# Prepare stage of a state-space and attention kernel: x split between the statistics pass and the first channel group, and filter taps made with the powers as the moving operand

## The reference

```
def _layernorm(x):   m = mean(x, -1); v = var(x, -1); return (x - m) / sqrt(v + 1e-5)
# first layer, a diagonal state-space model per channel d with 64 states n
A_bar = exp(DT * -exp(log_A));  B_bar = (A_bar - 1) / A * B_param
K[d, t] = sum_n C[d, n] * B_bar[d, n] * A_bar[d, n] ** t        # the filter taps
y = causal convolution of layernorm(x) with K, + D * layernorm(x);   x2 = x + y
# second layer: windowed attention, plus routed attention over 512 and 1024 chosen rows
```

## Time and profile before

| | us |
|---|---|
| Median of three runs | 4485.69 |
| Profiled execution: its time, its span | 4487.98, 4486.3 |
| Prepare block: 0 to first work of conv_phase | 144.0 |
| of it: to the start of taps and statistics | 11.3 |
| of it: loop of 32 steps | 11.3 to 121 |
| of it: end of the statistics, `krow`, store, end of block | 121 to 144 |
| conv_phase and what lies around it | 144 to about 620 |
| the rest | to 4486.3 |

### The profile page before, as it was taken

The page is one execution under the profiler, slowest core; times in us unless marked ns, Lnnn a source line. Parts: engine busy times, 40 slices in busy tenths (PEclk is TensorE's granted clock), DMA queues, the critical chain, the costliest instruction groups (busy, mean ns, idle before and its releaser), DMA issues. The chain is left out here.

```text
span 4486.3 us, 94318 instructions
## 1 busy us (share of the span) xinstructions
PE 4223.0 (94%) x37156; PEld 3557.5 (79%) x37156; DVE 2888.1 (64%) x4994; ACT 1852.9 (41%) x4838; POOL 869.6 (19%) x661
## 2 busy tenths in 40 slices
PE   9688879999999999999999999689999999999999
PEld 9577767888888888878888888577878777777777
DVE  7788867776676666755555666746465564655645
ACT  6334424343443434434444333225344453444534
POOL 0122202222222222222222222210110101111101
PEclk9999979999999999999999999869999999999999
DMA  9778852222222322212121211220210202112010
GB/s 306 217 201 230 225 160 76 90 79 89 83 90 82 90 86 84 79 50 65 58 67 58 63 62 46 90 57 6 50 40 21 55 8 50 25 36 46 16 42 13
DMA packets 341117, 369.20 MB, mean 82 GB/s; under 512 B 22848, under 2 KB 220736, under 8 KB 340672
## 3 DMA queue, kind: packets, MB, share of 16 engines
q1 hardware_dynamic: 262336, 295.91, 22.2%
q0 software_dynamic: 12288, 33.56, 3.6%
q10 hardware_dynamic: 66048, 33.56, 2.8%
HBM read 236.60 MB, written 76.02 MB: 70 GB/s over the span
## 5 line engine op out<-in xcount | busy, mean ns | idle before, releaser
L1685 POOL TENSOR_TENSOR l_prob<-l_prob,l_inv 128x768 f32<-128x768 f32 x256 | 389.6, 1543 | 1699.0 <-DVE l_inv L1642 1699.0
L1236 ACT ACTIVATE l_prob<-l_ps_s,l_neg_max 128x192 f32<-128x192 f32 x1024 | 420.7, 443 | 7.9 <-DVE l_neg_max L1618 7.7
L2296 DVE TENSOR_REDUCE h_neg_max<-h_ps_s 128x1 f32<-128x1024 f32 x256 | 312.8, 1222 | 166.6 <-PE h_ps_s L2082 163.4
L2217 ACT ACTIVATE h_prob<-h_ps_s,h_neg_max 128x1024 f32<-128x1024 f32 x256 | 285.5, 1115 | 292.5 <-DVE h_neg_max L2299 292.5
L1618 DVE TENSOR_REDUCE l_neg_max<-l_ps_s 128x4 f32<-128x768 f32 x256 | 233.1, 952 | 237.6 <-PE l_ps_s L1005 218.7
L2094 PE MATMUL h_ps_t<-ident,h_prob 128*128 128x128 f32 x2048 | 272.8, 276 | 14.4 <-ACT h_prob L2217 13.9
L2094 PEld LDWEIGHTS h_ps_t<-ident,h_prob 128*128 128x128 f32 x2048 | 228.3, 140 | 62.6 <-issue 27.7
L2106 PEld LDWEIGHTS h_ps_o<-h_probs_t,ahead_then_values 128*64 128x64 f32 x4096 | 220.9, 137 | 43.2 <-issue 37.0
L2106 PE MATMUL h_ps_o<-h_probs_t,ahead_then_values 128*64 128x128 f32 x4096 | 251.8, 276 | 0.0
L2353 DVE COPY h_probs_t<-h_ps_t 128x512 f32<-128x512 f32 x256 | 176.8, 691 | 115.8 <-PE h_ps_t L2094 114.3
L1236 ACT ACTIVATION_READ_ACCUMULATOR l_prob<-l_ps_s,l_neg_max 128x1 f32 x1024 | 235.2, 230 | 0.0
(11 more groups left out here) (384 smaller groups left out, 11222.3 us busy)
## 6 DMA issues: line engine op xcount, KB each, us to landing
xin<-in_L_attn_x_dram SPq DMA_DIRECT2D x32, 1024.0 KB, 5.1
xg<-in_L_attn_x_dram SPq DMA_DIRECT2D x64, 512.0 KB, 9.4
toep_back<-taps_padded ACTq DMA_DIRECT2D x32, 1024.0 KB, 10.6
x<-xg SPq DMA_DIRECT2D x64, 512.0 KB, 8.1
l_xin<-x SPq DMA_DIRECT2D x128, 256.0 KB, 3.2
l_xres<-x SPq DMA_DIRECT2D x128, 256.0 KB, 3.1
l_val_side<-l_val SPq DMA_DIRECT2D x256, 128.0 KB, 3.1
out_dram<-l_res SPq DMA_DIRECT2D x128, 256.0 KB, 2.0
```

Of the source, the lines that this page charges most:

```text
L1236: last = nc.scalar.activation(prob[t % 2][:, h, pair, :], ps_s[:, h, pair, BOTH], ACT.Exp, bias=neg_max[:, t % 2, h, pair:pair + 1], accum ...
L1685: nc.gpsimd.tensor_tensor(mine, mine, spread(inv[:, t % 2, h, :], [1, PAIRS], [0, WIN + P]), ALU.mult).then_inc(p_normed, 1)
L2217: nc.scalar.activation(prob[i % 2][:, :].rearrange("p (a k) -> p a k", a=2), ps_s[i % 2][:, :, :], ACT.Exp, bias=neg_max[:, qt % 2, h:h + ...
L2296: nc.vector.tensor_reduce(at, ps_s[i % 2][:, :, :].rearrange("p a k -> p (a k)"), AX_X, ALU.max, negate=True).then_inc(max_step, 1)
```

## The change

- The x loads: each load of 4 tiles becomes two DMAs, channels 128 to 511 into `xin` (now 384 wide) and channels 0 to 127 straight into their place in `first_group`. The 16 DMAs that loaded the first group afterwards go, and so does DVE's wait for them in conv_phase.
- bn_stats runs twice on each tile, on 128 and on 384 elements, and finish_stats combines four partial means and variances in place of two.
- Taps: stationary is now `cb_wide`, 32 columns for each pair of channels (16 pairs make a block of 32 channels; a pair's two columns hold its coefficients, the other 30 are zero), and moving are the 128 columns of powers. The 16 matmuls of a block accumulate in the same 32 partitions of PSUM, which thus hold 32 channels with time along the row. The copies to `taps_t` and the transposes go; `krow` is copied from four PSUM banks at the end.
- `cb_wide` (8192 elements in each partition) lies in room that conv_phase uses later, and POOL clears all of it.

```diff
-        xin = [sb(f"xin{i}", [P, tiles_per_load, DIM]) for i in range(4)]
-        bn = sb("bn", [P, TILES, 6])
+        xin = [sb(f"xin{i}", [P, tiles_per_load, DIM - P]) for i in range(4)]
+        bn = sb("bn", [P, TILES, 2, 6])
...
-                    sp.dma_start(xin[t % 4][:, :, :],
-                                 x_rows[:, t * tiles_per_load:(t + 1) * tiles_per_load, :]).then_inc(x_in[t % 4], 16)
-                load_group_part(sp, x, first_group, first_in, 0, range(NCH))
+                    tiles, b, c = slice(t * tiles_per_load, (t + 1) * tiles_per_load), t // 4, t % 4 * tiles_per_load
+                    sp.dma_start(xin[t % 4][:, :, :], x_rows[:, tiles, P:DIM]).then_inc(x_in[t % 4], 16)
+                    sp.dma_start(first_group[:, c:c + tiles_per_load, b, :], x_rows[:, tiles, 0:P]).then_inc(x_in[t % 4], 16)
...
-                nc.gpsimd.memset(cb_two[:, :, :], 0.0).then_inc(iota_made, 1)
+                nc.gpsimd.memset(cb_wide[:, :, :, :], 0.0).then_inc(iota_made, 1)
...
-                        wait(pe, taps_kept, s2 * 2 + par - 1)
-                        for q in range(SPAIRS):
-                            last = nc.tensor.matmul(ps_taps[par][:, 2 * q:2 * q + 2], powers[par][:, q, :],
-                                                    cb_two[:, columns((s2 * 2 + par) * SPAIRS + q, 1), :],
-                                                    start=True, stop=True)
...
-                    last = nc.tensor.transpose(ps_rows[:, g, :], taps_t[:, g * P:(g + 1) * P], ident[:, :])
+                for s in range(NSUB):
+                    pe.wait_ge(powers_made, s + 1)
+                    for q in range(s * SPAIRS, (s + 1) * SPAIRS):
+                        block, at = q // BLOCK, q // BLOCK * 2 * BLOCK
+                        last = nc.tensor.matmul(ps_rows[at // P][at % P:at % P + 2 * BLOCK, 0:P], cb_wide[:, block, q % BLOCK, :],
+                                                powers[s % 2][:, q % SPAIRS, :], start=(q % BLOCK == 0), stop=(q % BLOCK == BLOCK - 1),
+                                                skip_group_check=True)
+                    last.then_inc(taps_made, 1)
...
-                            nc.vector.bn_stats(bn[:, bass.ds(t4 * 16 + i * tiles_per_load + n, 1), :],
-                                               xin[i][:, n, :]).then_inc(stats_done, 1)
-                        v.wait_ge(taps_made, t4 * 4 + i + 1)
-                        nc.vector.tensor_copy(taps_t[:, bass.ds((t4 * 4 + i) * SUB, SUB)],
-                                              ps_taps[i % 2][:, 0:SUB]).then_inc(taps_kept, 1)
+                            at = bass.ds(t4 * 16 + i * tiles_per_load + n, 1)
+                            nc.vector.bn_stats(bn[:, at, 0, :], first_group[:, i * tiles_per_load + n, bass.ds(t4, 1), :])
+                            nc.vector.bn_stats(bn[:, at, 1, :], xin[i][:, n, :]).then_inc(stats_done, 1)
...
-                v.wait_ge(rows_turned, 1)
-                nc.vector.tensor_copy(krow[:, :, 0:CHUNK], ps_rows[:, :, ::-1]).then_inc(dve, 1)
+                v.wait_ge(taps_made, NSUB)
+                for g in range(KC):
+                    last = nc.vector.tensor_copy(krow[:, g, 0:CHUNK], ps_rows[g][:, CHUNK - 1::-1])
...
-                v.wait_ge(x_in[0], 16 * NCH)
```

More of the change, by code:

```diff
@@ L15 @@
 AX_X = mybir.AxisListType.X
+AX_XY = mybir.AxisListType.XY
 P = 128
@@ L82, in load_group_part, with prepare_phase @@
         sp.dma_start(to[:, c], x_v[c, :, :, g * P:(g + 1) * P]).then_inc(done, 16)
-def prepare_phase(nc, x, log_A, B_param, C, D, keep, kpad, first_group, first_in, new_sem, spent):
+BLOCK = 16
+def prepare_phase(nc, x, log_A, B_param, C, D, keep, kpad, first_group, cb_wide, new_sem, spent):
     tiles_per_load = 4
@@ L98, in sem @@
             return spent["prepare"][-1]
-        xin = [sb(f"xin{i}", [P, tiles_per_load, DIM]) for i in range(4)]
-        bn = sb("bn", [P, TILES, 6])
+        xin = [sb(f"xin{i}", [P, tiles_per_load, DIM - P]) for i in range(4)]
+        bn = sb("bn", [P, TILES, 2, 6])
+        sums = sb("sums", [P, TILES, 2])
+        gaps = sb("gaps", [P, TILES, 2, 2])
         raw = sb("raw", [P, 3, 2, P])
@@ L113, in prepare_phase @@
         ps_t = ps("ps_t", [P, 3, 4, P])
-        ps_taps = [ps(f"ps_taps{i}", [P, 512]) for i in range(2)]
-        ps_rows = ps("ps_rows", [P, KC, P])
+        ps_rows = [ps(f"ps_rows{i}", [P, 512]) for i in range(KC)]
         x_in = [sem(f"x_in{i}") for i in range(4)]
@@ L181, in _ @@
                 pe.wait_ge(cb_made, 1)
-                def taps_of_two(s2):
-                    for par in range(2):
-                        pe.wait_ge(powers_made, s2 * 2 + par + 1)
-                        wait(pe, taps_kept, s2 * 2 + par - 1)
-                        for q in range(SPAIRS):
-                            last = nc.tensor.matmul(ps_taps[par][:, 2 * q:2 * q + 2], powers[par][:, q, :],
-                                                    cb_two[:, columns((s2 * 2 + par) * SPAIRS + q, 1), :],
-                                                    start=True, stop=True)
[L190 to L194, removed]
-                    last = nc.tensor.transpose(ps_rows[:, g, :], taps_t[:, g * P:(g + 1) * P], ident[:, :])
-                last.then_inc(rows_turned, 1)
+                for s in range(NSUB):
[6 more added lines that the diff above has]
+                    last.then_inc(taps_made, 1)
             @block.scalar
@@ L237, in _ @@
                 v.wait_ge(iota_made, 3)
-                nc.vector.tensor_copy(cb_two[0:STATE, :, 0], cb[0:STATE, :]).then_inc(dve, 1)
-                nc.vector.tensor_copy(cb_two[STATE:P, :, 1], cb[STATE:P, :]).then_inc(cb_made, 1)
+                wide = cb_wide[:, :, :, :].rearrange("p a q n -> p a (q n)")
+                nc.vector.tensor_copy(wide[0:STATE, :, 0::2 * BLOCK + 2], cb[0:STATE, :].rearrange("p (a q) -> p a q", q=BLOCK)).then_inc(dve, 1)
+                nc.vector.tensor_copy(wide[STATE:P, :, 1::2 * BLOCK + 2], cb[STATE:P, :].rearrange("p (a q) -> p a q", q=BLOCK)).then_inc(cb_made, 1)
                 v.wait_ge(dve, 9)
@@ L243, in _ @@
                     for i in range(4):
-                        v.wait_ge(x_in[i], t4 * 16 + 16)
+                        v.wait_ge(x_in[i], t4 * 32 + 32)
                         for n in range(tiles_per_load):
-                            nc.vector.bn_stats(bn[:, bass.ds(t4 * 16 + i * tiles_per_load + n, 1), :],
-                                               xin[i][:, n, :]).then_inc(stats_done, 1)
-                        v.wait_ge(taps_made, t4 * 4 + i + 1)
-                        nc.vector.tensor_copy(taps_t[:, bass.ds((t4 * 4 + i) * SUB, SUB)],
-                                              ps_taps[i % 2][:, 0:SUB]).then_inc(taps_kept, 1)
-                v.wait_ge(stats_done, TILES)
-                finish_stats(nc, v, dve, 9, bn, mean, rstd, tmp, tmp2, sqrt_done)
-                v.wait_ge(rows_turned, 1)
-                nc.vector.tensor_copy(krow[:, :, 0:CHUNK], ps_rows[:, :, ::-1]).then_inc(dve, 1)
+                            at = bass.ds(t4 * 16 + i * tiles_per_load + n, 1)
+                            nc.vector.bn_stats(bn[:, at, 0, :], first_group[:, i * tiles_per_load + n, bass.ds(t4, 1), :])
+                            nc.vector.bn_stats(bn[:, at, 1, :], xin[i][:, n, :]).then_inc(stats_done, 1)
+                v.wait_ge(stats_done, TILES)
+                finish_stats(nc, v, dve, 9, bn, sums, gaps, mean, rstd, tmp, tmp2, sqrt_done)
+                v.wait_ge(taps_made, NSUB)
+                for g in range(KC):
+                    last = nc.vector.tensor_copy(krow[:, g, 0:CHUNK], ps_rows[g][:, CHUNK - 1::-1])
+                last.then_inc(dve, 1)
                 v.wait_ge(dve, 9 + FINISH_STEPS + 1)
@@ L259, in _, with finish_stats @@
                                         spread(dcol[:, :], [1, KC], [1, 1]), ALU.add).then_inc(krow_made, 1)
-FINISH_STEPS = 11
-def finish_stats(nc, v, chain, n, bn, mean, rstd, tmp, tmp2, sqrt_done):
-    half = DIM // 2
+FINISH_STEPS = 14
+def finish_stats(nc, v, chain, n, bn, sums, gaps, mean, rstd, tmp, tmp2, sqrt_done):
     def step(ins):
@@ L274, in step @@
         v.wait_ge(chain, n)
[L276 to L282, removed]
-                                        op0=ALU.mult, op1=ALU.add))
-    nc.vector.tensor_scalar(tmp[:, :], tmp[:, :], EPS, None, ALU.add).then_inc(sqrt_done, 1)
+    rest = DIM // P - 1
+    step(nc.vector.tensor_tensor(sums[:, :, :], bn[:, :, :, 1], bn[:, :, :, 4], ALU.add))
+    step(nc.vector.scalar_tensor_tensor(out=mean[:, :], in0=sums[:, :, 1], scalar=float(rest), in1=sums[:, :, 0],
+                                        op0=ALU.mult, op1=ALU.add))
+    step(nc.vector.tensor_scalar(mean[:, :], mean[:, :], 0.5 * P / DIM, None, ALU.mult))
+    step(nc.vector.tensor_tensor(gaps[:, :, :, :], bn[:, :, :, 1::3], spread(mean[:, :], [1, TILES], [0, 2], [0, 2]), ALU.subtract))
```

(12 more changed lines are left out.)

6 lines of the change are left out of this document (1 added, 5 removed).

## The result

Four runs of the changed kernel took 4449.6 to 4456.42 us, median 4454.89; four of the kernel before on the same chip 4479.52 to 4491.22, median 4486.04. The ratio is 0.9934, with a 95% interval of 0.9921 to 0.9947: 31 us faster by the medians, between 24 and 35 by the interval. The forecast was 4462 and its whole range 4454 to 4474.

A forecast was written before the change was run, and what follows sets the result against it. PE was taken to pace the prepare loop, then the `krow` store waited behind queued loads. Loop 15.5 and queue about 13 gained, finish_stats and copies 3.7 lost: 24.6 us earlier, forecast 4462, own range 4457 to 4467, whole 4454 to 4474.

The forecast's parts named there:

- finish_stats: After the prepare loop: combining four partial statistics takes 5.6 us, 3.2 more than before, and the rest 2.6.
- four copies and D: End of the prepare block: four copies of 128 elements take 1.1 us instead of 0.7, the step with D 0.2.
- PE off the path, ACT sets the taps, DVE the loop: Prepare loop: PE falls to 2.05 us a step, under ACT's 2.44; taps end near 92 to 95, DVE's statistics at 105.3.
- The end of the block: After the statistics: `krow` ready at 115.2, its store meets an empty queue and lands in 3.7 us, conv_phase starts at 119.4.
- Statistics on DVE: Prepare loop: two bn_stats take 709 ns a tile, 90.8 us for 128 tiles, 93.0 in all; bounds 79.1 and 108.
- Loads: DMA in the prepare loop: 1536- and 512-byte pieces take 93 ns a row, 95.5 us in all, last landing near 101.5.
- POOL's clear: Loop start: the 7.0 us clear of `cb_wide` holds DVE by 1.0 us, start 12.3; bounds nothing, or 1.7 plus 0.9.
- a hold of over 2 us: Loop start: L226's successor on DVE held for over 2 us was listed as showing the prediction wrong.
- Rival 1: Prepare loop: loads bind, statistics end at 113.5, conv_phase at 127.4, 16.6 us earlier, time 4471; chance 0.15.
- Rival 2: Taps: PE stays at the slow clock, 3.4 us a step, conv_phase at 127.2, 16.8 us earlier, time 4471; chance 0.14.
- Rival 3: Taps: matmuls accumulating into the same 32 partitions do not overlap, 352 ns a record, 54 us later, time 4540; chance 0.05.
- Rival 4: After the block: conv_phase waits for something else and gives the gain back, time about 4485; chance 0.08.

The follow-up runs named there:

- the run with 128 columns: Kernel before with each taps matmul streaming 128 coefficient columns instead of 2, stationary still 128 x 128; 4459.02 us (one run), conv_phase starts at 123.1.
- the run with half of the stream: Changed kernel with only 64 of the 128 columns of powers streamed, taps 64 to 127 left out; 4455.65 us (one run), conv_phase starts at 113.7.
- the x-only run: Changed kernel with the old taps put back, keeping the split x loads and double bn_stats; 4472.2 us, ratio 0.9971, conv_phase starts at 133.8.
- the split clear: Changed kernel with DVE clearing half of `cb_wide` while idle and POOL the other half; 4452.76 us (one run), conv_phase starts at 112.1.
- the last version: Kernel before with new taps, `cb_wide` clear shared by DVE and POOL, POOL copying the first group from whole-tile loads; 4440.85 and 4441.62 us, ratios 0.9902 and 0.9904.
- the run with 64 columns: Kernel before with each taps matmul streaming 64 coefficient columns instead of 2, stationary still 128 x 128; 4487.78 us (one run), conv_phase starts at 142.9.

## Why the prediction was right, step by step

| step | predicted | measured |
|---|---|---|
| start of the loop | 12.3 | 13.8 |
| loop, with the loads | 93.2 | 85.8 |
| finish_stats | 8.4 | 8.0 |
| four copies and D | 1.3 | 1.1 |
| store and end of block | 4.2 | 4.0 |
| conv_phase starts | 119.4 | 112.7 |

- **PE off the path, ACT sets the taps, DVE the loop: right.** The reason given, that the clock would be fast with the full stream, held too: the run with 128 columns shows it with the old weight load. In the runs with 2 columns, and even with 64, beside that load the pace stayed at 214 ns for 109 us. What the prediction did not name is that the narrow load frees PE as well (the run with half of the stream).
- **The end of the block: right.** With no second load of the group and no queue ahead of the store, the store and the end of the block came out within 0.2 us, and finish_stats within 0.4; the x-only run isolates them.
- **Statistics on DVE: the term that was mis-sized.** Worked out were 709 ns a tile and 93.0 us in all, measured 656 and 85.8. I gave 91 ns to each instruction from a copy out of PSUM and a step of 4 elements. The two bn_stats are 0.197 and 0.459 us apart: 1.02 ns an element and 66 ns an instruction. The second instruction thus costs 38 ns over the 618 of one, not 91. The start of conv_phase came 6.7 us earlier than worked out: 7.4 less in the loop, 7.2 of it this term, 1.5 more at its start and 0.8 less behind it.
- **Loads: too slow by 8%** (93 ns a row for 86). **Rival 1** (the loads bind, statistics at 113.5) is out, but it was near: DVE's real pace was faster than worked out, and the loads alone end the statistics at about 99.1 against DVE's 99.7. Both terms were too large by about 8%, and with a margin that small it is in part luck that DVE came out as the one that binds.
- **POOL's clear: too small.** 1.0 us was taken. DVE's step was held 2.3 us, until both clears were through, and the loop started 2.5 us later than before, near the upper bound of 2.6; a hold of over 2 us was one of the signs I had named for wrong. My own said as much: there the DVE step began 1.59 us before POOL's ended and took 1.46 us longer than alone. The Trainium skill, "SBUF — State Buffer" (SBUF: two separate sides), has an exclusive lock on the shared pair of ports, held for the whole instruction. Rows 8, the 2.63 us here and the split clear's 0.29 us agree with it better than with the value that I took. It was worth 2.1 us at the start of the loop and 0.6 at its end, where DVE meets the pace of the loads.
- **Rival 2** (slow clock): out for the full stream, 110 ns a record after the first 32; with half a stream it rose and fell. **Rival 3** (no overlap of accumulating matmuls): out, 110 ns a record and not 352. **Rival 4** (given back later): out, within what the rest varies by.

## What to carry to other kernels

Ask of a PE-bound loop how much each matmul streams, and at which pace its records run. Here 2 columns against a full stationary operand cost 214 ns a record, and both swapping the operands (110 ns) and widening the stream to 128 columns (128 ns) took PE off the path. When one bound goes, work out the next two with their own rows. Here DVE and the loads lay within 1 us of each other, so that an edit of DVE's start alone brought 0.6 us; the last version won 9 to 10 by moving both, and 3 of them by the shorter finish_stats. Before a load is split for two consumers, see whether an idle engine can copy the second one's part: here POOL's 32 copies of 0.6 to 0.7 us cost nothing that shows.

## What was not expected of the hardware

- The granted clock in the windows view is 1.00 over the old loop and over the run with 64 columns, while every record runs at the pace of the slow level (214 ns a record, durations 352 and 421 ns). In all runs the column stands at 1.00 from the start of the trace, and reads 0.50 only after PE has run at the fast pace and then been idle. In the first stretch of these traces the level had to be read from the pace of the records.
- One bn_stats of 512 elements follows the next after 618 ns, while 128 and 384 elements together take 656: by 1.02 ns an element and 66 ns an instruction, an estimate from these two shapes, one of 512 should take 590.
- 512-byte pieces ran at 269 to 292 GB/s as whole group loads, and in pairs with 1536-byte ones at 383 together. Why the group loads are slower was not tested.
